# One line group moved in TensorE's order: the step's piece of projection between logits and row logits

## The chip, the cores and the metric

The kernel runs as one program on 1 core of a Trainium2 chip. The metric is the device time of one execution in microseconds (us), lower is better, given as the median of several runs.

## The reference, cut to what matters

A decoder layer on 8 batches of 256 rows with 512 columns: a retention layer, then a cross attention, then a mixture-of-experts feed forward, each with a layernorm in front and the residual added. All arithmetic is float32. The change lies in the cross attention alone:

```python
q = (x @ Wq).reshape(b, n, 32, 16)                 # x: the normalised rows
k, v = split(ctx @ Wkv)                            # 32 heads of 16
q, k = apply_axial_rope(q, pos), apply_axial_rope(k, pos)
w = softmax(einsum('bqhd,bkhd->bhqk', q, k) / 4)
attn = einsum('bhqk,bkhd->bqhd', w, v).reshape(b, n, 512)
x = x + attn @ Wout + bout
```

## The kernel before

The cross attention is a software pipeline written out by hand. Heads are worked two at a time: a batch g has 16 pairs p, and one pair is one **step**. An iteration b of the outer loop has T = 16 steps i, and in each step every engine does some work for up to four batches (`live` lists which). Iteration 0 starts batch 0 and prepares batch 1; iterations 1 to 6 are full; iteration 7 prepares no new batch; iteration 8 only drains.

What TensorE does, by function:

- `rows(g, p)` at step p: the row logits of a pair, four matmuls of 256 columns with 50 rows (L1254), into two banks of `b_rt`. VectorE's `maximum` reduces them to row maxima (L1471), and `rows` of the next step waits for that reduce.
- `logits(g, p)` 8 steps later (LAGS): the transposed logits with the maximum folded in (L1268), into the other two banks of `b_rt`. ScalarE's `exponentials` reads them (L1631), and the next `logits` waits for it.
- `values(g, q)`, 11 steps after the rows (LAGV), in odd steps: the products with v for four heads (L1281), copied out by ScalarE (`values_out`, L1624).
- `turn_values(g, q)`, one step later, in even steps: transposes of the result (L1289); VectorE's `group` divides by the sums and writes `b_attn` (L1491, L1493).
- `turn_maxima(g, k)`, in steps 4, 8, 12 and 0: transposes of the negated maxima (L1295); ScalarE copies them to `b_mT` (L1620) and DMAs place them beside q.
- `use(g, what, n, parts)`: one **piece** of a projection or of the output. `PLAN` says which piece stands in which step; step numbers are taken modulo 16, so all 16 steps of a full iteration have one. Step 4 has the two transposes of the normalised rows, `x0` and `x1` (L1311), step 5 `k1`, step 11 the two transposes of the attention result, `o0` and `o1` (L1339), step 12 `v0`. The others are parts of q, k, v and of the output w. The matmuls are made by `matmul3`, three fp32r products a term (L41, L42, L43).

All pieces share two PSUM banks, `b_gm`, in turns: w1, x0, k1, q1, o1, v1 in bank 0 and k0, x1, q0, o0, v0, w0 in bank 1. The first part of a piece waits for `gm_read` of its bank, that is, until the piece before it there has been read. The readers work in the following step: `take` on VectorE multiplies k and q by the rotary tables (L1461, twice), adds w to the residual (L1467) and forms the low parts `b_xl` of x and o (L1453) after ScalarE has written the high parts `b_xh` (L1594, L1599). `x0` waits besides for `xn_done`, the rows normalised by VectorE in steps 2 and 3 (L1441), and `o0` for `attn_done`, the last `group` of step 10.

The order within a step is fixed by the program of each engine. VectorE's is: `take` of the previous step's piece, `maximum`, `negate` (in steps 3, 7, 11 and 15), `group` (even steps), then statistics and `normalize`. ScalarE's is: `take`, `exponentials`, the high part of a rotated k or q, `maxima_out`, `values_out`. SyncE's queue issues the chunk loads of q and k, the maxima and the write-outs of the rotated rows, in steps of the same count.

Of the kernel before, what the change touches and what calls it, by code (L numbers as in the profile page):

```python
# [1021 lines left out]
def cross_attention(nc, X, Wa, Wb, first, csT, wb_dram, ctx_dram, bout_dram, pack_dram, ident, held, final, lead, ws_dram, gate_dram, const_dram, tri_dram):  # L1022
# [6 lines left out]
    with ExitStack() as mem:  # L1029
# [37 lines left out]
        def pb(name, shape):  # L1067
# [28 lines left out]
        PLAN = [(32, "w", 1, (0, 1)), (33, "w", 1, (2,)), (34, "w", 1, (3,)), (-14, "k", 0, (0,)), (-13, "k", 0, (1,)),  # L1096
# [16 lines left out]
        def uses(g, what, n):  # L1113

            place = [use[1:] for use in ORDER].index((what, n))
            ahead = ORDER[place][0] // T
            total, per = 0, 0
            for m, use in enumerate(ORDER):
                if m % 2 == place % 2:
                    more, done = ahead - use[0] // T + (m <= place), int(use[1] in AHEAD)  # L1120
                    if isinstance(g, int):
                        total += max(min(g + more, B) - done, 0)
                    else:
                        total, per = total + more - done, per + 1
            return total if isinstance(g, int) else g * per + total

        def due(i, live, step):

            return [d for d in live if i - d * T == step]

        def pairs(i, live, lag):
            return [(d, i - d * T - lag) for d in live if 0 <= i - d * T - lag < HP]

        def quads(i, live, lag):
            return [(d, (i - d * T - lag) // 2) for d in live if 0 <= i - d * T - lag < HP and (i - d * T - lag) % 2 == 0]
# [17 lines left out]
        def fresh(g):  # L1153
            return isinstance(g, int) and g <= 0

        def second(g):
            return isinstance(g, int) and g == 1
# [84 lines left out]
        def _(pe):  # L1242
# [14 lines left out]
            def logits(g, p):  # L1257

                k = p // 4
                if p % 4 == 0:  # L1260
                    pe.wait_ge(m_moved[k % 2], g * 128 + (k // 2 * 64 + 64))
                if fresh(g) and p == 0:
                    pe.wait_ge(mx_done, LAGS + 1)
                pe.wait_ge(e_done, g * HP + (p + 1))
                for j in range(TB):
                    for e in range(2):
                        r = slice(64 * e, 64 * e + 3 * XD + 2)
                        last = nc.tensor.matmul(rt[:, 2 + e, j * S:(j + 1) * S], kT[r, p, j * P:(j + 1) * P], qT[r, p, :], start=True, stop=True)  # L1268
                last.then_inc(st_mm, 1)
# [28 lines left out]
            def use(g, what, n, parts):  # L1298
                bank = BANK[what, n]
                out = gm[:, bank, :]  # L1300
                a = slice(n % 2 * P, (n % 2 + 1) * P)
                if 0 in parts:
                    earlier = uses(g, what, n) - 1
                    if not (isinstance(earlier, int) and earlier == 0):
                        pe.wait_ge(gm_read[bank], earlier)
                if what == "x":
                    if n == 0:
                        pe.wait_ge(xn_done, g)
                    rows_n = first.xn if second(g) else xn
                    for m in range(KT):  # L1310
                        last = nc.tensor.transpose(out[:, m * P:(m + 1) * P], rows_n[:, n, m * P:(m + 1) * P], ident[:, :])  # L1311
                elif what == "k":
                    if 0 in parts:
                        pe.wait_ge(cl_done, g)
                    for r in parts:
                        for m in range(CKT):
                            o = m * 2 * C + (2 * r + n) * P
                            last = matmul3(nc, out[:, r * S:(r + 1) * S], (wh[:, 1, o:o + P], wl[:, 1, o:o + P]),
                                           (ch[:, m, :], cl[:, m, :]), m == 0, m == CKT - 1)
                elif what == "q":  # L1320
                    if n == 0 and 0 in parts:
                        for t in range(TB):
                            pe.wait_ge(gm_read[BANK["x", t]], uses(g, "x", t))
                    for part in parts:
                        r = part // 2
                        for m in range(part % 2 * 2, part % 2 * 2 + 2):
                            o = m * C + (2 * r + n) * P
                            last = matmul3(nc, out[:, r * S:(r + 1) * S], (wh[:, 0, o:o + P], wl[:, 0, o:o + P]),
                                           (xh[:, m, :], xl[:, m, :]), m == 0, m == KT - 1)
                elif what == "v":  # L1330
                    for m in parts:
                        o = (2 * m + 1) * C
                        last = matmul3(nc, out, (ch[:, m, a], cl[:, m, a]), (wh[:, 1, o:o + C], wl[:, 1, o:o + C]),
                                       m == 0, m == CKT - 1)
                elif what == "o":
                    if n == 0:
                        pe.wait_ge(attn_done, g * 8 + 9)
                    for m in range(KT):
                        last = nc.tensor.transpose(out[:, m * P:(m + 1) * P], attn[:, n, m * P:(m + 1) * P], ident[:, :])  # L1339
                else:  # L1340
                    if 0 in parts:
                        pe.wait_ge(wl_done, 1)
                        pe.wait_ge(gm_read[BANK["o", n]], uses(g, "o", n))
                    for m in parts:
                        last = matmul3(nc, out, (ah[:, m, a], al[:, m, a]), (wh[:, 2, m * C:(m + 1) * C], wl[:, 2, m * C:(m + 1) * C]),
                                       m == 0, m == KT - 1)
                if PARTS[what] - 1 in parts:
                    last.then_inc(gm_mm[bank], 1)
# [35 lines left out]
            def body(b, live):  # L1384
                for i in range(T):
                    for d, p in pairs(i, live, LAGS):
                        logits(b + d, p)
                    for d, p in pairs(i, live, 0):
                        rows(b + d, p)
                    if isinstance(b, int) and b == 0 and i == 1:  # L1390
                        for n in range(8):
                            nc.tensor.transpose(nat[:, 0:P], ident[:, :], ident[:, :])
                    for d, q in quads(i, live, LAGV + 1):
                        turn_values(b + d, q)
                    for k in range(4):
                        for d in due(i, live, 4 * k + 4):
                            if not (fresh(b + d) and k == 0):
                                turn_maxima(b + d, k)
                        for d in due(i, live, 4 * k + 5):
                            pe.wait_ge(mt_done, (b + d) * 4 + (k + 1))  # L1400
                    if isinstance(b, int) and b == B and 4 <= i < 8:
                        lead_turn(i - 4)
                    if isinstance(b, int) and b == B and i == 10:
                        lead_router((0, 1))
                    for d, q in quads(i, live, LAGV):
                        values(b + d, q)
                    for step, what, n, parts in PLAN:
                        for d in due(i, live, step):
                            if not (fresh(b + d) and step < 0):
                                use(b + d, what, n, parts)  # L1410
                    if isinstance(b, int) and b == 0 and i == 4:
                        turn_maxima(0, 0)
                    if isinstance(b, int) and b == B and i == 11:
                        lead_router((2, 3))
                    if isinstance(b, int) and b == B and i == 12:
                        lead_turn_later(4)
                        lead_turn_later(5)
# [1320 lines left out]
```

## Time and profile before

| | us |
|---|---|
| median of 3 runs | 1372.47 (1368.34 to 1374.85) |
| the profiled execution, its time | 1369.42 |
| its span in the profile | 1367.6 |
| mean granted TensorE clock | 0.99 of full speed |
| TensorE busy with matmuls | 1329.1 |
| VectorE busy | 824.3 |
| ScalarE busy | 486.6 |

The cross attention runs from about 346.8 us of the span, where the first row logits start, to a little past 700 us. PE is TensorE's matmul, PEld its weight load, DVE VectorE, ACT ScalarE. Each matmul of the table of instructions overlaps the next, so a busy PE says that matmuls are in flight, not that the array is streaming all the time; the distance from one start to the next is what counts.

### The profile page before, as it was taken

How to read it: one execution, taken by the hardware profiler on the slowest of the kernel's cores; microseconds unless marked ns; L12 is line 12 of the kernel's file. 1: busy time of each engine (PE TensorE's matmuls, PEld its weight loads, DVE VectorE, ACT ScalarE, POOL GpSimd, SP SyncE). 2: the span in 40 equal slices, each digit the busy share in tenths (PEclk: the TensorE clock that was granted, in tenths of full speed). 3: DMA queues.
4: the chain of work that ended last, by engine and by line, in shares of the span. 5: the costliest groups of instructions: out<-in, count | busy, mean ns of one | idle time of the engine just before them, and what ended most of it. 6: DMA issues, size and time to landing. Idle time of an engine off the chain costs nothing. (4 is left out here: it accounts for less than half of the span.)

```text
span 1367.6 us, 24216 instructions
## 1 busy us (share of the span) xinstructions
PE 1329.1 (97%) x8490; PEld 1076.7 (79%) x8490; DVE 824.3 (60%) x1494; ACT 486.6 (36%) x765; POOL 519.9 (38%) x371
## 2 busy tenths in 40 slices
PE   8999999998889999999989999999999999999997
PEld 7777788877667777777568788888888899999986
DVE  6766667789777888888844657555531222222248
ACT  4222333334366665666665111111111232222220
POOL 1122222225543443344142018441133686555074
PEclk9999999999899999999999999999999999999999
DMA  7992000002655545555400003240010544443257
GB/s 273 321 327 104 0 0 0 0 9 94 185 163 167 173 144 152 157 150 172 126 1 23 24 24 146 85 150 24 23 39 1 195 148 143 143 175 111 85 172 245
DMA packets 85036, 159.85 MB, mean 117 GB/s; under 512 B 8576, under 2 KB 61952, under 8 KB 81536
## 3 DMA queue, kind: packets, MB, share of 16 engines
q1 hardware_dynamic: 78688, 124.19, 28.6%
q0 software_dynamic: 6272, 34.61, 7.1%
q8 instruction: 52, 0.85, 0.3%
q14 instruction: 24, 0.20, 0.1%
HBM read 109.22 MB, written 69.47 MB: 131 GB/s over the span
## 5 line engine op out<-in xcount | busy, mean ns | idle before, releaser
L1631 ACT ACTIVATE b_pf<-b_rt,b_zero 128x1024 f32<-128x1024 f32 x128 | 142.9, 1116 | 104.3 <-PE b_rt L1268 103.8
L1471 DVE TENSOR_REDUCE b_mx<-b_rt 128x4 f32<-128x1024 f32 x128 | 156.3, 1222 | 37.4 <-PE b_rt L1254 36.8
L2192 DVE SCALAR_TENSOR_TENSOR residual<-c_yp,c_shared,residual 128x512 f32<-128x512 f32 x128 | 92.3, 745 | 104.9 <-PE c_yp L43 100.8
L41 PE MATMUL c_fc<-c_xh,c_w 128*128 128x512 f32 x348 | 136.0, 391 | 0.0
L43 PE MATMUL c_fc<-c_xh,c_w 128*128 128x512 f32 x348 | 135.5, 389 | 0.0
L42 PE MATMUL c_fc<-c_xl,c_w 128*128 128x512 f32 x348 | 135.4, 389 | 0.0
L2358 ACT ACTIVATE c_s<-c_fc 128x512 f32<-128x512 f32 x43 | 25.7, 598 | 228.5 <-PE c_fc L43 217.4
L2206 DVE TENSOR_TENSOR c_hTl<-c_eh,c_hTh 128x384 fp32r<-128x384 f32 x39 | 21.8, 558 | 140.5 <-ACT c_hTh L2382 128.2
L41 PE MATMUL c_fc<-c_ring,c_xTl 128*128 x312 | 104.0, 333 | 0.0
L43 PE MATMUL c_fc<-c_ring,c_xTh 128*128 x312 | 100.7, 323 | 0.0
L42 PE MATMUL c_fc<-c_ring,c_xTh 128*128 x312 | 100.3, 322 | 0.0
L2003 POOL TENSOR_TENSOR c_w<-c_wraw,c_zero 128x1536 fp32r<-128x1536 f32 x9 | 24.7, 2749 | 197.3 <-DMA c_wraw<-in_c_ws 108.1
L2025 POOL TENSOR_TENSOR c_ring<-c_eraw,c_ring 128x2816 fp32r<-128x2816 f32 (+1 forms) x16 | 78.2, 4885 | 1.3
L2023 POOL TENSOR_TENSOR c_ring<-c_eraw,c_zero 128x2816 fp32r<-128x2816 f32 (+1 forms) x16 | 61.1, 3816 | 46.2 <-DMA c_eraw<-in_c_we 46.2
L43 PEld LDWEIGHTS c_fc<-c_xh,c_w 128*128 128x128 f32 x348 | 65.3, 188 | 13.6
L41 PEld LDWEIGHTS c_fc<-c_xh,c_w 128*128 128x128 f32 x348 | 65.3, 188 | 13.4
L42 PEld LDWEIGHTS c_fc<-c_xl,c_w 128*128 128x128 f32 x348 | 65.3, 188 | 13.3
L1268 PE MATMUL b_rt<-weights_b 50*128 50x256 f32 x512 | 65.1, 333 | 9.4 <-DMA weights_b<-b_mT 5.2
L1268 PEld LDWEIGHTS b_rt<-weights_b 50*128 50x128 f32 x512 | 38.6, 186 | 41.8 <-issue 20.9
L1281 PE MATMUL b_av<-b_pf,b_vp 128*32 128x256 f32 x1024 | 69.4, 389 | 0.0
L2388 ACT COPY c_ye<-c_ey 128x512 f32<-128x512 f32 x39 | 22.9, 587 | 119.5 <-PE c_ey L43 119.5
L41 PEld LDWEIGHTS c_fc<-c_ring,c_xTl 128*128 128x128 f32 x312 | 58.7, 188 | 3.5 <-issue 0.8
(451 smaller groups left out, 3543.2 us busy)
## 6 DMA issues: line engine op xcount, KB each, us to landing
weights_b<-b_pack SPq DMA_DIRECT2D x128, 200.0 KB
c_eraw<-in_c_we POOLq DMA_DIRECT2D x8, 2176.0 KB, 9.9
b_pack<-b_hi SPq DMA_DIRECT2D x56, 256.0 KB, 2.5
c_rows_in<-in_b_ctx SPq DMA_DIRECT2D x39, 256.0 KB, 10.3
c_rows_out<-in_b_ctx SPq DMA_DIRECT2D x39, 256.0 KB, 10.5
c_xe<-c_rows_in SPq DMA_DIRECT2D x39, 256.0 KB, 2.7
c_rows_out<-c_ye SPq DMA_DIRECT2D x39, 256.0 KB
c_wraw<-in_c_ws SPq DMA_DIRECT2D x11, 768.0 KB, 4.3
```

The costliest lines, as they stand in the source:

```text
L41: nc.tensor.matmul(out, ll, rh, start=start, stop=False)
L42: nc.tensor.matmul(out, lh, rl, start=False, stop=False)
L43: return nc.tensor.matmul(out, lh, rh, start=False, stop=stop)
L1268: last = nc.tensor.matmul(rt[:, 2 + e, j * S:(j + 1) * S], kT[r, p, j * P:(j + 1) * P], qT[r, p, :], start=True, stop=True)
L1281: last = nc.tensor.matmul(av[r:r + VW, 0:S], vp[:, j * XH + h, :], pf[:, h % 8, j * S:(j + 1) * S], start=j == 0, stop=j == TB - 1)
L1471: nc.vector.tensor_reduce(out=mx[:, :, 2 * p:2 * p + 2].rearrange("p t e -> p e t"), in_=rt[:, row_bank(g, p):row_bank(g, p) + 2, :].rearr ...
L1631: nc.scalar.activation(pf[:, s:s + 2, :], rt[:, 2:4, :], ACT.Exp, scale=XD ** -0.5, bias=zero[:, :]).then_inc(e_done, 1)
L2003: nc.gpsimd.tensor_tensor(w[k][:, 0, :], wraw[k][:, 1, :], zero[:, :].to_broadcast([P, PW]), ALU.add).then_inc(high_done, 1)
L2023: nc.gpsimd.tensor_tensor(high, raw, zero[:, :].to_broadcast([P, hi - lo]), ALU.add).then_inc(high_done, 1)
L2025: nc.gpsimd.tensor_tensor(low, raw, as_f32(high), ALU.subtract).then_inc(ew_done, 1)
L2192: nc.vector.scalar_tensor_tensor(out=X[:, t, :], in0=yp[:, (n * 4 + k) % 3, :], scalar=shared[:, t:t + 1], in1=X[:, t, :], op0=ALU.mult, o ...
L2358: nc.scalar.activation(s[:, n % 2, :], fc[:, n % 2, 0, :] if n else lead.products[:, 0, :], ACT.Silu).then_inc(s_done, 1)
```

## The change

In each step TensorE's `use` stands directly behind `logits` and ahead of `rows`, `turn_values`, `turn_maxima` and `values`. Before, it stood behind all of them. No instruction is added or removed on any engine, and no engine other than TensorE has another order.

```diff
                 for i in range(T):
                     for d, p in pairs(i, live, LAGS):
                         logits(b + d, p)
+                    for step, what, n, parts in PLAN:
+                        for d in due(i, live, step):
+                            if not (fresh(b + d) and step < 0):
+                                use(b + d, what, n, parts)
                     for d, p in pairs(i, live, 0):
                         rows(b + d, p)
                     if isinstance(b, int) and b == 0 and i == 1:
...
                     for d, q in quads(i, live, LAGV):
                         values(b + d, q)
-                    for step, what, n, parts in PLAN:
-                        for d in due(i, live, step):
-                            if not (fresh(b + d) and step < 0):
-                                use(b + d, what, n, parts)
                     if isinstance(b, int) and b == 0 and i == 4:
                         turn_maxima(0, 0)
```

## Rows read from the trace of the kernel before

**Rows 1.** The page: TensorE's busy time and granted clock

```profile
PE 1329.1 (97%) x8490; PEld 1076.7 (79%) x8490; DVE 824.3 (60%) x1494; ACT 486.6 (36%) x765; POOL 519.9 (38%) x371
PEclk9999999999899999999999999999999999999999
```

**Rows 2.** The waits of PE: us in total, times, longest

```profile
PE b_rt L1268 <- ACT b_pf L1631: 3.4, 7, 0.6
PE b_rt L1254 <- DVE b_mx L1471: 1.0, 3, 0.5
```

**Rows 3.** Timeline of PEld, steps 0 and 1: start, us, engine

```profile
562.86 0.30 PEld L1268 LDWEIGHTS b_rt<-weights_b 50*128 50x128 f32 x4 [0.37 <-issue]
...
563.52 0.20 PEld L1289 LDWEIGHTS b_nat<-identity,b_at 128*128 128x128 f32 x2
...
563.91 0.19 PEld L41 LDWEIGHTS b_gm<-weights_a,b_xl 128*128 128x128 f32 x1
...
565.50 0.30 PEld L1268 LDWEIGHTS b_rt<-weights_b 50*128 50x128 f32 x4 [0.36 <-issue]
565.73 0.30 PEld L1254 LDWEIGHTS b_rt<-weights_b 50*128 50x128 f32 x4
566.17 0.59 PEld L1281 LDWEIGHTS b_av<-b_pf,b_vp 128*32 128x32 f32 x16
567.17 0.19 PEld L41 LDWEIGHTS b_gm<-weights_a,b_xl 128*128 128x128 f32 x1 [0.41 <-issue]
...
568.06 0.30 PEld L1268 LDWEIGHTS b_rt<-weights_b 50*128 50x128 f32 x4 [0.36 <-issue]
```

**Rows 4.** Timeline of PEld in iteration 8, logits with no row logits behind

```profile
684.93 0.30 PEld L1268 LDWEIGHTS b_rt<-weights_b 50*128 50x128 f32 x4 [0.36 <-issue]
685.37 0.20 PEld L1289 LDWEIGHTS b_nat<-identity,b_at 128*128 128x128 f32 x2
```

**Rows 5.** Timeline of PEld, last transposes of step 4, logits of step 5

```profile
573.93 0.25 PEld L1295 LDWEIGHTS b_av<-identity,b_nm 128*128 128x128 f32 x2
...
574.93 0.42 PEld L1311 LDWEIGHTS b_gm<-identity,b_xn 128*128 128x128 f32 x4 [0.31 <-DVE b_bs L1461]
575.52 0.30 PEld L1268 LDWEIGHTS b_rt<-weights_b 50*128 50x128 f32 x4 [0.17 <-issue]
```

**Rows 6.** Timeline of DVE: reduce of step 1, then steps 3 to 5

```profile
566.29 1.23 DVE L1471 TENSOR_REDUCE b_mx<-b_rt 128x4 f32<-128x1024 f32 x1 [0.24 <-PE b_rt L1254]
...
571.50 1.21 DVE L1471 TENSOR_REDUCE b_mx<-b_rt 128x4 f32<-128x1024 f32 x1
...
573.59 0.69 DVE L1461 TENSOR_TENSOR b_ac<-b_gm,table 128x512 f32<-128x512 f32 x1
...
574.79 1.22 DVE L1471 TENSOR_REDUCE b_mx<-b_rt 128x4 f32<-128x1024 f32 x1
...
576.37 1.28 DVE L1453 TENSOR_TENSOR b_xl<-b_gm,b_xh 128x512 fp32r<-128x512 f32 x2
```

**Rows 7.** Timeline of ACT: steps 15 and 4

```profile
561.41 0.37 ACT L1624 COPY b_at<-b_av 128x256 f32<-128x256 f32 x1 [0.15 <-PE b_av L1281]
...
574.66 0.34 ACT L1620 CAST b_mT<-b_av 32x256 fp32r<-32x256 f32 x1
575.04 1.17 ACT L1594 CAST b_xh<-b_gm 128x512 fp32r<-128x512 f32 x2
```

**Rows 8.** Timeline of PE: two long waits for the maxima's DMAs

```profile
376.21 0.50 PE L1268 MATMUL b_rt<-weights_b 50*128 50x256 f32 x4 [2.18 <-DMA weights_b<-b_mT]
...
388.55 0.50 PE L1268 MATMUL b_rt<-weights_b 50*128 50x256 f32 x4 [3.01 <-DMA weights_b<-b_mT]
```

**Rows 9.** Windows: busy us of PE, PEld, DVE, ACT, POOL, clock, DMA

```profile
376.00:378.00 2.00, 1.78 (x15) 1.57 (x16) 1.00 (x1) 1.24 (x2) 0.00 (x0) 1.00 0.95 316
...
388.00:390.00 2.00, 1.45 (x11) 1.22 (x12) 0.54 (x1) 0.90 (x1) 0.00 (x0) 0.75 0.77 247
...
394.00:396.00 2.00, 2.00 (x13) 1.78 (x12) 1.36 (x3) 1.11 (x1) 1.88 (x2) 0.54 0.51 146
```

## The prediction

> **What bounds the kernel now.** I read the page first: TensorE is busy for 97% of the span, and its granted clock is at or near full in all forty slices [rows 1]. The change touches TensorE's order in the cross attention alone, so the question is what TensorE spends there. The view of the waits gives it little: 3.4 us on ScalarE's exponentials and 1.0 us on VectorE's maxima in the whole kernel [rows 2]. So TensorE sets the pace of the attention, and a step is as long as its TensorE work. What can make it longer is work that overlaps less, or new waits.
>
> Next the weight loads in order of time, since each opens a block of matmuls [rows 3]. Step 0 runs from 562.86 to 565.50 = 2.64 us, step 1 from 565.50 to 568.06 = 2.56 us. From the logits' first load to the transposes (563.52) are 0.66 us for logits and row logits together, from the transposes to the piece (563.91) 0.39 us, from the piece to the next logits 1.59 us. In step 1 the values take 1.00 us (566.17 to 567.17) and the piece 0.89 us. The piece is the last block of a step. Everything that VectorE and ScalarE do for it ahead of time has the whole step to be finished, and this is the reserve that the change spends.
>
> **First part: more switches between kinds of blocks.** No instruction goes or comes, but neighbours change. Logits and row logits have the same shape and flow into each other: 0.66 us for both. Logits followed by another kind take 0.44 us until the next load (684.93 to 685.37) [rows 4]; row logits followed by another kind take the same 0.44 us (565.73 to 566.17) [rows 3]. With the piece between them both pay it: together 0.86 to 0.88 us against 0.66, so 0.20 us more in each step. A piece behind logits costs what it costs behind values or transposes (0.89 and 1.59 us, first load to next load), I assume, and values behind row logits stay as they are. In even steps the transposes now stand directly before the next logits. Today the piece's loads run on from them (0.39 us for four transposes). A block of transposes before logits shows a gap: the last four transposes of step 4 load for 0.42 us, then 0.17 us pass, and logits load at 575.52 [rows 5]. So even steps pay 0.20 + 0.17 = 0.37 us. Eight even and eight odd steps: 8 x 0.37 + 8 x 0.20 = 4.6 us for a full iteration. The bounds are 0 (if the loads are pulled ahead, and I see no row of that here) and 16 x 0.37 = 5.9 us.
>
> The Trainium skill, "TensorE: Matmul & The Clock Gate", section "Step-by-step: what each phase is for", says that TensorE pulls weight loads ahead of matmuls in flight where row groups do not conflict or where the background weight buffer takes them. By that alone the switches would cost nothing, and the sum below would be about 30 us less. The rows disagree for this pair of shapes: before each logits behind a piece the loader is idle for 0.36 us.
>
> **Second part: pieces whose inputs come from the step before.** The piece is now wanted 0.43 us after the step's start. Row logits, and with them the reduce and all that VectorE has behind it, move to the far side of the piece, so the end of the chain moves later too. A chain of VectorE that begins with the reduce of the previous step can start about 0.55 us after the first load of the row logits (565.73 to 566.29) [rows 3, 6]. I count from that load, R, and compare it with the moment at which TensorE comes to the piece. A reduce takes 1.2, reduce and `group` 1.58 (574.79 to 576.37), `take` of k or q 1.20 (573.59 to 574.79), one half of `b_xl` 0.6 us [rows 6]. Four pieces of an iteration are late:
>
> - x1, step 4. It needs k0 read from bank 1. VectorE has reduce, `negate`, `normalize` and `take` k0 in a row: from the reduce at 571.50 to the load of x1 at 574.93 are 3.43 us [rows 5, 6], with no gap in it. The start is R + 0.55, or R + 1.1 if `take` of w1 is still ahead of it. So x1 can start at R + 4.0 to 4.5. TensorE arrives after row logits 0.43, values 1.00, logits 0.43 and x0 0.43, at R + 2.3. Stall 1.7 to 2.2; I take 2.0 us. `xn_done` of x0 lies inside this wait.
> - k1, step 5. It needs the low half of x0. ScalarE serves the maxima first: from their load to the copy 0.73 us and to the high part 1.11 us (573.93, 574.66, 575.04) [rows 5, 7]. These transposes load at R + 0.60, so the high part starts at R + 1.7 and is there at R + 2.3; with 0.6 for the low half, k1 can start at R + 3.0. TensorE arrives at R + 0.43 + 0.56 + 0.43 = 1.4. Stall 1.5 us.
> - o0 and o1, step 11. `group` of step 10 ends at R + 0.55 + 1.58 = 2.1, and o0 is wanted at R + 0.43 + 0.34 + 0.43 = 1.2. Behind `group` VectorE takes q1, 1.2 us, and only then bank 0 is free for o1: R + 3.45 against R + 1.6. Stall 1.8 us, the one of o0 inside it.
> - v0, step 12. It needs the low half of o0. ScalarE first copies out the values of step 11, which now end with the step: R + 1.43, then 0.14 until the copy starts (its row shows 0.15 of waiting) and 0.4 for the copy (0.37 and a little) [rows 7], 0.6 high, 0.65 low: R + 3.25 against R + 1.86. Stall 1.4 us.
>
> Together 6.7 us. For the other pieces the bank was last written two steps before, or the input is older; I find no wait there. Today's steps 4 and 5 already wait, 0.31 us for x1 [rows 5] and about as much for the maxima, and that is contained in the new stalls, so 0.7 us comes off. What is late next is the row logits of the same step, and VectorE idles for them; VectorE then has spare time, so this does not go on growing. SyncE's queue changes little: the maxima leave up to 1.5 us later in steps 5, 9, 13 and 1, and the logits that need them come three steps later.
>
> **The sum.** A full iteration: 6.7 - 0.7 + 4.6 = 10.6 us. Six of them (1 to 6; in iteration 1 the output pieces of two steps are missing, 0.6 us less): 63. Iteration 0 has six steps with all three blocks (1.9 us) and the stalls of x1 and k1, but two waits for DMAs of 2.18 and 3.01 us end near its last steps [rows 8] and can swallow part of it: 3 us, between 0 and 6. Iteration 7 has six pieces, 1.7 us, and o0 for about 1 us; the drain 0.4 us. Sum 63 + 3 + 2.7 + 0.4 = 69 us. On the profiled execution of 1369.4 us that is 1438; its time lies 3 us under the median of the three runs, and on the median it is 1441. I take 1439. A measurement of this kernel can tell 0.5%, some 7 us, from no change.
>
> **Rivals.**
> - The stalls also bring the clock down. The wait of 2.18 us before 376.21 left the granted clock at full speed (1.00 from 376 to 378); the one of 3.01 us before 388.55 was followed by windows at 0.75 down to 0.50 [rows 8, 9], the lower level of 1.2 GHz, until about 396. Six to seven us at half speed cost about 3.5. Once in an iteration is 6 x 3.5 = 21 us more, 1460; at all four places it would be over 1500. My longest gap is shorter than the one that left the clock alone, but four come in every iteration. The Trainium skill, same page, section "A second HAM failure mode: psum-queue depth-cycling", says that frequent short idling between groups of matmuls can make the clock oscillate; no row here shows it for gaps of this length.
> - The stalls are hidden and only the switches cost. That needs VectorE to be ahead by two us and more at steps 4 and 11. The rows speak against it, since its chain of steps 3 to 5 has no gap. It gives 1369 + 6 x 4.6 + 4 = 1401.
> - The switches cost nothing and only the stalls remain: 1369 + 6 x 6.0 + 4 = 1409. The idle loader before logits speaks against it.
> - Not slower. The row logits now come later, when the reduce of the previous step is surely over, and VectorE and ScalarE can read a piece while TensorE is at rows and values. What that can win is TensorE's waits on them, 3.4 + 1.0 us, with x1's 0.3 under 5 us: 1364, which would be measured as no change. It decides only if switches cost under 0.04 us a step and no piece is late. I see four that are.
>
> **How the numbers follow.** Forecast 0.62, with its own range 1415 to 1458; clock 0.13; stalls hidden 0.11; switches free 0.09; not slower 0.05. The range 1396 to 1466 takes in the second and third rival and the mild form of the first, and leaves out its strong form and the last. Slower by over 0.5% 0.94, within 0.5% 0.04 (nearly all of the last rival), faster 0.02.
>
> **What the profile after would show.** A full iteration about 10 us longer than before, 53 to 54 us where 16 steps of 2.6 to 2.7 us take 42 to 44 now. The waits of PE: on L1461 at the load of x1 near 2 us six or seven times, on L1453 at the first load of k1 and of v0 near 1.5 us each, on L1461 at o1. The loads of row logits 0.43 us ahead of values or transposes and the same from logits to the piece. VectorE's idle time before the reduce, on L1254, several times as large. In the windows of the attention TensorE busy falls from all but full to about 85%. A wait of PE on a line that I do not name, a clock under full speed in the middle of the attention, or iterations only 5 us longer would show me wrong: the first a chain that I overlooked, the second the clock, the third one of the two middle rivals.

## The result, and the profile after

The changed kernel takes 1462.16 us (median of 4 runs, 1456.29 to 1463.41), the kernel before 1370.81 us beside it: 1.065 times, 95% interval 1.062 to 1.068. The forecast of 1439 was 23 us short, inside its range of 1396 to 1466. The likeliest case was not quite what happened. It was that case together with the first rival.

The page, its share of busy time and the clock in forty slices, to be held against [rows 1]:

```profile
PE 1378.3 (94%) x8490; PEld 1094.0 (75%) x8490; DVE 823.7 (56%) x1494; ACT 487.5 (33%) x765; POOL 516.7 (35%) x371
PEclk9999999998998988899999999999999999999999
```

VectorE and ScalarE have the same instructions and, within 1 us, the same busy time. Busy time of TensorE grew by 49 us, and six slices between the 10th and the 20th show a clock under nine tenths, where before one did: the same matmuls, some at the lower level. The rest of the 94 us by which the span grew is idle time.

The view of TensorE's waits (us in all, times, longest), where [rows 2] had 4.4 us on two lines:

```profile
PE b_gm L41 <- DVE b_xl L1453: 16.1, 13, 1.7
PE b_gm L1311 <- DVE b_xn L1441: 9.7, 6, 1.8
PE b_gm L1339 <- DVE b_attn L1493: 6.4, 7, 1.1
PE b_gm L1311 <- DVE b_bs L1461: 5.5, 6, 3.3
PE b_rt L1268 <- ACT b_pf L1631: 5.1, 8, 1.0
...
PE b_rt L1254 <- DVE b_mx L1471: 3.2, 6, 1.1
PE b_gm L1339 <- DVE b_bs L1461: 3.2, 6, 0.5
```

The lines on `b_gm`, the pieces, are the forecast's four places and no others: k1 and v0 wait for `b_xl` 13 times, x0 for the normalised rows and x1 for the bank of k0, o0 for the last `group` and o1 for the bank of q1. They come to 41 us. Logits and row logits (`b_rt`) wait a little more too, 5.1 and 3.2 us where [rows 2] had 3.4 and 1.0.

The timeline of the weight loads in steps 14, 15, 3, 4 and 5 of one iteration, as in [rows 3, 5] (pieces' inner loads left out):

```profile
617.02 0.30 PEld L1268 LDWEIGHTS b_rt<-weights_b 50*128 50x128 f32 x4 [0.41 <-issue]
617.45 0.19 PEld L41 LDWEIGHTS b_gm<-weights_a,b_cl 128*128 128x128 f32 x1
...
619.70 0.30 PEld L1254 LDWEIGHTS b_rt<-weights_b 50*128 50x128 f32 x4 [0.35 <-issue]
620.13 0.20 PEld L1289 LDWEIGHTS b_nat<-identity,b_at 128*128 128x128 f32 x2
620.50 0.30 PEld L1268 LDWEIGHTS b_rt<-weights_b 50*128 50x128 f32 x4 [0.17 <-issue]
...
635.38 0.30 PEld L1268 LDWEIGHTS b_rt<-weights_b 50*128 50x128 f32 x4 [0.41 <-issue]
637.62 0.42 PEld L1311 LDWEIGHTS b_gm<-identity,b_xn 128*128 128x128 f32 x4 [1.95 <-issue]
638.76 0.42 PEld L1311 LDWEIGHTS b_gm<-identity,b_xn 128*128 128x128 f32 x4 [0.72 <-DVE b_bs L1461]
639.34 0.30 PEld L1254 LDWEIGHTS b_rt<-weights_b 50*128 50x128 f32 x4 [0.17 <-issue]
...
640.36 0.30 PEld L1268 LDWEIGHTS b_rt<-weights_b 50*128 50x128 f32 x4 [0.17 <-issue]
642.20 0.19 PEld L41 LDWEIGHTS b_gm<-b_ch,weights_a 128*128 128x128 f32 x1 [1.54 <-DVE b_xl L1453]
...
645.26 0.30 PEld L1268 LDWEIGHTS b_rt<-weights_b 50*128 50x128 f32 x4 [0.41 <-issue]
```

Logits to piece take 0.43 us, row logits to transposes 0.43, two transposes to the next logits 0.37, as forecast. Step 4 lasts from 635.38 to 640.36 = 4.98 us, step 5 until 645.26 = 4.90.

What VectorE does meanwhile, timeline of DVE in steps 3 and 4:

```profile
635.32 1.21 DVE L1471 TENSOR_REDUCE b_mx<-b_rt 128x4 f32<-128x1024 f32 x1
636.66 0.18 DVE L1482 TENSOR_SCALAR b_nm<-b_mx 128x16 fp32r<-128x16 f32 x1
...
636.97 0.54 DVE L1441 TENSOR_SCALAR b_xn<-residual,b_mv,b_rstd 128x512 f32 x1
637.42 0.69 DVE L1461 TENSOR_TENSOR b_ac<-b_gm,table 128x512 f32<-128x512 f32 x1
638.02 0.68 DVE L1461 TENSOR_TENSOR b_bs<-b_gm,table 128x512 f32<-128x512 f32 x1
639.89 1.23 DVE L1471 TENSOR_REDUCE b_mx<-b_rt 128x4 f32<-128x1024 f32 x1 [1.19 <-PE b_rt L1254]
```

The reduce of step 3 starts at 635.32 and x1 is released at 638.76, 3.44 us later; before it was 3.43 [rows 5, 6]. From there on the chain is the same, it only starts too late, and then VectorE idles 1.19 us for the row logits that stand behind x1.

The starts of all 128 logits give the length of each step. Full iterations at full clock (us):

| step | before | changed | | step | before | changed |
|---|---|---|---|---|---|---|
| 0 | 2.64 | 3.05 | | 8 | 2.83 | 3.08 |
| 1 | 2.56 | 2.77 | | 9 | 2.57 | 2.77 |
| 2 | 2.45 | 2.83 | | 10 | 2.46 | 2.86 |
| 3 | 2.57 | 2.77 | | 11 | 2.69 | 4.68 |
| 4 | 2.43 | 4.98 | | 12 | 2.75 | 4.39 |
| 5 | 3.60 | 4.90 | | 13 | 2.57 | 2.76 |
| 6 | 2.47 | 2.86 | | 14 | 3.12 | 3.48 |
| 7 | 2.57 | 2.77 | | 15 | 3.27 | 3.46 |

Twelve steps are 3.4 us longer together, by 0.2 (odd) or 0.25 to 0.4 us (even). The four with late pieces are 7.5 us longer. That is 10.8 us an iteration (54.4 against 43.6), where the forecast had 10.6.

What is missing is the clock. Steps 4 and 5 were slower still in four of the six full iterations. The windows about one such place (busy us of PE, PEld, DVE, ACT, POOL; then clock, DMA share, GB/s):

```profile
514.00:518.00 4.00, 2.13 (x24) 0.98 (x16) 3.83 (x8) 1.49 (x2) 0.00 (x0) 0.93 0.64 171
518.00:522.00 4.00, 3.60 (x16) 2.43 (x16) 1.80 (x4) 0.78 (x3) 1.41 (x2) 0.50 0.11 24
522.00:526.00 4.00, 3.16 (x14) 2.94 (x16) 1.29 (x2) 2.06 (x4) 1.28 (x1) 0.50 0.17 56
526.00:530.00 4.00, 4.00 (x36) 2.58 (x34) 2.42 (x3) 1.49 (x2) 0.96 (x2) 0.79 0.41 144
```

The stall before x0 had just ended:

```profile
517.12 0.78 PE L1311 MATMUL b_gm<-identity,b_xn 128*128 128x128 f32 x4 [1.77 <-DVE b_xn L1441]
```

From about 517.5 to 527.7 (worked out from the shares 0.93 and 0.79 of the outer windows) the clock was granted at one half, 1.2 GHz. Steps 4 and 5 of this iteration took 13.2 us instead of 9.9. In two iterations step 11 was slow as well, in one of them step 12 too, and the waits there were far shorter:

```profile
543.83 0.66 PE L1339 MATMUL b_gm<-identity,b_attn 128*128 128x128 f32 x4 [0.96 <-DVE b_attn L1493]
545.02 1.12 PE L1339 MATMUL b_gm<-identity,b_attn 128*128 128x128 f32 x4 [0.54 <-DVE b_bs L1461]
545.00:547.00 2.00, 1.98 (x12) 1.42 (x16) 0.09 (x1) 0.00 (x0) 1.41 (x2) 0.50 0.29 106
```

### The profile page after: what moved, and what is told of

Read it like the earlier page. It is cut to its first block and busy times, and to the rows that moved or that the text cites. A ratio compares the mean times of both kernels' runs of the same rounds, so it can differ in the third digit from the quotient of the medians.

```text
span 1461.6 us, 24218 instructions
## 1 busy us (share of the span) xinstructions
PE 1378.3 (94%) x8490; PEld 1094.0 (75%) x8490; DVE 823.7 (56%) x1494; ACT 487.5 (33%) x765; POOL 516.7 (35%) x371
## 5 line engine op out<-in xcount | busy, mean ns | idle before, releaser
L1268 PEld LDWEIGHTS b_rt<-weights_b 50*128 50x128 f32 x512 | 39.8, 192 | 48.6 <-issue 36.4
L1268 PE MATMUL b_rt<-weights_b 50*128 50x256 f32 x512 | 66.5, 339 | 8.8 <-ACT b_pf L1631 5.1
L1254 PE MATMUL b_rt<-weights_b 50*128 50x256 f32 x512 | 68.2, 347 | 5.7 <-DVE b_mx L1471 3.2
L1281 PE MATMUL b_av<-b_pf,b_vp 128*32 128x256 f32 x1024 | 73.4, 407 | 0.0
L1254 PEld LDWEIGHTS b_rt<-weights_b 50*128 50x128 f32 x512 | 41.3, 200 | 35.4 <-issue 20.7
## 6 DMA issues: line engine op xcount, KB each, us to landing
c_rows_in<-in_b_ctx SPq DMA_DIRECT2D x39, 256.0 KB, 10.6
```

Of the source, the lines that this page charges most:

```text
L1254: last = nc.tensor.matmul(rt[:, row_bank(g, p) + e, t * S:(t + 1) * S], qT[r, p, t * P:(t + 1) * P], kT[r, p, :], start=True, stop=True)
L1281: last = nc.tensor.matmul(av[r:r + VW, 0:S], vp[:, j * XH + h, :], pf[:, h % 8, j * S:(j + 1) * S], start=j == 0, stop=j == TB - 1)
```

## The experiments

Each kernel ran in rounds with the kernel before on the same chip. Ratios are to that kernel; its median was between 1365 and 1371 us. Step lengths are taken from the starts of the logits, as above.

**Twelve pieces moved, four left (e1).** The pieces of steps 4, 5, 11 and 12 stay at the end of their step.

```diff
+        LATE = (4, 5, 11, 12)
...
                         logits(b + d, p)
+                    for step, what, n, parts in PLAN:
+                        for d in due(i, live, step):
+                            if not (fresh(b + d) and step < 0) and (step % T not in LATE):
+                                use(b + d, what, n, parts)
...
-                            if not (fresh(b + d) and step < 0):
+                            if not (fresh(b + d) and step < 0) and (step % T in LATE):
```

> The pieces of twelve steps stand between logits and row logits, those of steps 4, 5, 11 and 12 stay at the end of their step. My theory (switches between kinds of blocks cost by themselves, stalls come only at the four): no new waits and no lower clock, but 8 odd or even steps pay 0.20 and 0.37 us, 3.5 us in a full iteration, some 23 us in all, so about 1394 us. Rival (the switches are hidden and all of the loss is stalls and clock): within 5 us of 1371.

Measured: 1402.99 us, 1.0257 times (1.0231 to 1.0283). The kernel before took 1367.01 us beside it, so the twelve cost 36 us, where my theory had 23 and the rival at most 5. The twelve steps have to a hundredth the lengths of the changed kernel, so 3.4 us an iteration is what the switches cost where nothing waits. The other 13 us are something that I had not thought of. Between step 3, whose piece is early, and step 4, whose piece is late, no piece stands between two row logits, and they come too fast for VectorE. The loads of step 4:

```profile
598.03 0.30 PEld L1269 LDWEIGHTS b_rt<-weights_b 50*128 50x128 f32 x4 [0.41 <-issue]
599.23 0.30 PEld L1255 LDWEIGHTS b_rt<-weights_b 50*128 50x128 f32 x4 [0.90 <-DVE b_mx L1476]
...
601.39 0.69 PEld L1312 LDWEIGHTS b_gm<-identity,b_xn 128*128 128x128 f32 x4 [0.72 <-DVE b_bs L1466]
```

Step 4 became 1.5 us, step 11 0.8 us and step 12 0.4 us longer through this. Switching costs are confirmed, and "nothing waits" was wrong for a mixed order. "No lower clock" was wrong too. In two of the six full iterations steps 4 and 5 took 8.8 us instead of 7.6. The windows behind the loads above, which belong to one of them:

```profile
601.00:603.00 2.00, 1.60 (x8) 1.28 (x10) 1.97 (x5) 1.06 (x2) 1.41 (x2) 0.61 0.26 62
603.00:605.00 2.00, 2.00 (x23) 0.94 (x20) 2.00 (x3) 1.73 (x3) 0.04 (x1) 0.53 0.01 4
```

The matmuls had waited 0.70 us for the maxima and 0.48 us at x1, nothing longer (the loader's 0.90 and 0.72 us count from its own last load).

**Four pieces moved, twelve left (e2).** The same with `in` and `not in` exchanged.

> Only the pieces of steps 4, 5, 11 and 12 are moved. My theory: 6.0 us of net stall and 1.1 us of switches in each of six iterations, some 5 us at the ends, and the clock falls to its lower level after some of the stalls as in the changed kernel, 20 us more: about 1438 us. Rival (the clock falls for another reason, such as the many short gaps at the twelve other places): no stretch at the lower level beyond those of the kernel before, 1419 us.

Measured: 1409.89 us, 1.0319 (1.0294 to 1.0345): 43 us, less than either theory. Step 4 took 3.45 us and not 4.98, because step 3 now ends with its piece and TensorE comes to x0 later, and step 11 likewise 3.47 and not 4.68. Steps 5 and 12 took 4.90 and 4.38 us as in the changed kernel, and step 13 0.6 us more than before for the mixed order. That is 5.4 us an iteration at full clock (49.0 against 43.6). In three of six iterations step 5 took 6.35 to 6.39 us, the lower clock again. So the clock does fall with these four alone, though less often.

**Twelve pieces at the very front (e3).** As e1, with the twelve ahead of the logits.

```diff
                 for i in range(T):
+                    for step, what, n, parts in PLAN:
+                        for d in due(i, live, step):
+                            if not (fresh(b + d) and step < 0) and (step % T not in LATE):
+                                use(b + d, what, n, parts)
                     for d, p in pairs(i, live, LAGS):
                         logits(b + d, p)
```

> As the first of these, but the twelve pieces stand ahead of the logits, at the very front of their step, so logits and row logits touch again and the piece is wanted even earlier. My theory (what costs there is the parting of the two, not the early place): 1371 us, within 5. Rival (a piece early in its step costs something at every step, by waits or by work pushed behind it): 1385 us or more.

Measured: 1392.57 us, 1.0191 (1.0159 to 1.0222). The total missed my 1371 and falls into the rival's range. The steps say why. Steps 6 to 9 have only moved pieces, and they take 1.75 + 3.37 + 1.97 + 3.29 = 10.4 us, as before (10.4) and unlike the changed kernel (11.5): with logits and row logits touching again, the switching cost is gone. What costs is the seam, as in e1: steps 3 and 4 together take 6.6 to 7.2 us in iterations 2 to 6 (5.0 before, and with one piece more in them), with waits of row logits for the reduce of up to 1.6 us. Behind these waits the clock fell in four of six iterations, which are 47.3 to 49.4 us long where the one after them has 46.9. The place in the step costs nothing by itself; an order that differs from step to step does.

**Work in the stalls (e4).** The changed kernel with matmuls ahead of the four late pieces.

```diff
+                                if step in (-12, -11, 27, -4) and n == (what == "k") and 0 in live and not fresh(b):
+                                    pe.wait_ge(mx_done, b * HP + (i + 1))
+                                    for _ in range(9):
+                                        nc.tensor.matmul(rt[:, 0, 0:S], wh[:, 0, 0:P], wh[:, 0, 0:S], start=True, stop=True)
                                 use(b + d, what, n, parts)
```

> The changed kernel with nine idle-time matmuls of 256 columns, 1.1 us together, ahead of the late piece in steps 4, 5, 11 and 12 of iterations 1 to 7 (their results are overwritten by the row logits). They wait for the maxima of the step before, so that their bank is free, which is over well before the piece's own input is there. My theory: the four stalls bring the clock down, and with work in them it stays up; 20 us faster than the changed kernel, about 1440 us. Rival (the clock has no part in it, the stalls are simply longer than forecast): no gain, 1462 us or slightly more.

Measured: 1434.91 us, 1.0502 (1.0468 to 1.0536). More matmuls made it 20 us faster than the change, by the two ratios. The windows of the attention, filled kernel:

```profile
420.00:500.00 80.00, 77.52 (x637) 53.42 (x640) 52.53 (x96) 40.47 (x59) 24.54 (x24) 1.00 0.43 127
500.00:580.00 80.00, 76.64 (x657) 54.62 (x650) 55.40 (x103) 39.52 (x57) 26.32 (x27) 1.00 0.40 120
580.00:660.00 80.00, 77.52 (x642) 53.75 (x640) 54.13 (x104) 40.93 (x59) 26.30 (x27) 1.00 0.45 131
```

and of the changed kernel:

```profile
420.00:500.00 80.00, 71.61 (x568) 48.18 (x566) 49.25 (x85) 38.77 (x57) 24.27 (x24) 0.94 0.44 130
500.00:580.00 80.00, 72.19 (x539) 47.73 (x539) 53.00 (x104) 36.10 (x50) 23.39 (x24) 0.87 0.38 110
580.00:660.00 80.00, 72.61 (x584) 49.68 (x582) 50.76 (x91) 38.32 (x55) 26.29 (x28) 0.92 0.39 115
```

In iterations 2 to 6 all late steps now have the length of the table above within 0.05 us, and these iterations are 54.5 us each, where the changed kernel has 57.4, 61.3, 59.2, 54.4 and 54.4. One stretch at the lower clock is left behind them, in iteration 7 (0.83 from 740 to 750 us).

**Only the wait (e9),** the control: `range(0)` in place of `range(9)`.

> The control for the filled kernel: the changed kernel with the same added wait for the maxima of the step before at the four late pieces, but no matmuls behind it. My theory (the matmuls keep the clock up, the wait is nothing): as the changed kernel, 1.065 times before, about 1460 us, with stretches at the lower clock in the attention. Rival (the added wait itself orders things better): as the filled kernel, 1.050 times.

Measured: 1456.63 us, 1.0687 (1.0646 to 1.0728). Iterations 2 to 6 are again 61.4, 59.2, 54.4, 54.4 and 57.4 us long. These are the lengths of the changed kernel's iterations, in another order. So the wait alone does nothing, and it is the matmuls that keep the clock up.

**All pieces first, filled (e5).** The loop over `PLAN` with the four added lines of e4 stands ahead of the logits.

> The filled kernel, but with every piece at the very front of its step, ahead of the logits, so that logits and row logits touch again and the pieces of steps 4, 5, 11 and 12 are wanted 0.43 us earlier still. My theory: the parting of logits and row logits with its switches costs 4.6 us in a full iteration, the four longer stalls give 4 x 0.43 = 1.7 us of it back, net 2.9 us x 6 = 17 us faster than the filled kernel, 1.038 times the kernel before, about 1420 us. Rival (switches cost nothing): 10 us slower than the filled kernel, 1.057 times the kernel before, about 1446 us.

Measured: 1438.04 us, 1.0497 (1.0464 to 1.0530), the same as e4 and between the two expectations. Steps 6 to 9 take 10.4 us, so the switching cost is gone here too. Iteration 4, the only one from 2 to 6 that stays at full clock, takes 52.9 us where e4 has 54.5: 1.6 us won, forecast 2.9. So the stalls grew by more than the 0.43 us that I added to each. From the logits of step 3 to those of step 4, which now include x0 and x1, are 6.6 to 7.5 us in iterations 2 to 6. The added matmuls themselves stand behind a wait for the maxima of up to 2.0 us:

```profile
PE b_rt L1393 <- DVE b_mx L1476: 22.9, 25, 2.0
```

So they leave the first part of the stall empty, and the clock fell in four of the six full iterations; these take 53.8 to 54.8 us. From iteration 1 on the attention is 4.0 us shorter than in e4. In these two executions what lies ahead of it and behind it is 2.5 and 3.3 us longer, and such stretches vary by more than that between executions of one order (see the ends, below). The total alone could not have told the theories apart.

**VectorE's order mended for k0 and the rows (e6).** TensorE as changed.

```diff
                     for step, what, n in ENDS:
-                        for d in due(i, live, step + 1):
+                        for d in due(i, live, step + (what in ("x", "o"))):
                             if not (fresh(b + d) and step < 0):
                                 take(b + d, what, n)
+                    for t in range(TB):
+                        for d in due(i, live, -14 + t):
+                            if not fresh(b + d) and not second(b + d):
+                                normalize(b + d, t)
                     for d, p in pairs(i, live, 0):
                         maximum(b + d, p)
...
-                    for t in range(TB):
-                        for d in due(i, live, -14 + t):
-                            if not fresh(b + d) and not second(b + d):
-                                normalize(b + d, t)
```

> TensorE's order as changed; VectorE takes k, q and w in the step of the piece itself instead of the next one, and normalises, both ahead of the reduce. My theory: the stall of x0 and x1 in step 4 (2.5 us) is VectorE's chain behind the late reduce, so it goes to under 0.5 us; k1, o0 and v0 keep theirs. 2.2 x 6 = 13 us, and one fewer cause for the lower clock, some 5 us: about 1444 us, 1.054 times before. Rival (the chain is not what x1 waits for, or the reduce becomes late by as much): within 5 us of the changed kernel, 1.065 times.

Measured: 1454.32 us, 1.0627 (1.0596 to 1.0658), barely better than the change and by the total the rival's case. The chain was what x1 waited for, but the gain went elsewhere, as the rival's second half had it. The waits of TensorE:

```profile
PE b_gm L41 <- DVE b_xl L1454: 16.3, 13, 1.7
PE b_gm L1340 <- DVE b_attn L1494: 11.0, 7, 1.8
PE b_rt L1255 <- DVE b_mx L1472: 9.6, 10, 1.8
...
PE b_gm L1312 <- DVE b_xn L1442: 1.9, 5, 0.4
```

The wait for the rows went from 9.7 to 1.9 us, the one of x1 for its bank is gone, and step 4 fell from 4.98 to 2.95 us. But the reduce of step 2 now stands behind w1's `take` and `normalize` and is late, so that the row logits of step 3 wait 0.7 to 0.9 us, and the take of q1 ahead of the reduce of step 10 delays the last `group`: o0 waits 11.0 us in all, where o0 and o1 together had 9.6. Step 11 keeps its 4.68 us in one of six iterations, and is 6.2 us or more in the others. One wait, 1.93 us for the loader and 1.7 us for the matmuls, has taken the place of two shorter ones, and the clock falls behind it:

```profile
593.73 1.47 PEld L1340 LDWEIGHTS b_gm<-identity,b_attn 128*128 128x128 f32 x8 [1.93 <-DVE b_attn L1494]
```

```profile
592.00:594.00 2.00, 0.28 (x4) 0.27 (x3) 1.65 (x4) 1.11 (x1) 1.61 (x3) 0.97 0.94 323
594.00:596.00 2.00, 2.00 (x12) 1.67 (x10) 0.00 (x0) 0.00 (x0) 0.00 (x0) 0.50 0.19 71
```

The first is the load of o0 and o1, the second the windows around it.

**Steps 4 and 5 alone (e7), steps 11 and 12 alone (e10).** As e2 with `LATE = (4, 5)` and `(11, 12)`.

> Only the pieces of steps 4 and 5 are moved. My theory: x1 2.0 and k1 1.5 us of stall less 0.7 of today's waits, 0.57 us of switches, 3.4 us in each of six iterations and 3 us in iteration 0: 23 us, 1392 us, and steps 11 and 12 would account for the other 20 of the 43 us that the four cost together. Rival (the cost of the four is mostly in one pair): under 10 or over 35 us.

> Only the pieces of steps 11 and 12 are moved, the other half of the four. The step lengths of the kernel with all four moved say 0.8 us more in step 11, 1.6 in step 12 and 0.6 in step 13, 3.0 x 6 = 18 us, and 2 to 3 us in iteration 7: 1391 us, 1.015 times before. Rival (the pairs do not add up, since each needs the other's delay or the clock): under 1.010 or over 1.022.

Measured: 1393.91 us, 1.0175 (1.0145 to 1.0205), and 1386.03 us, 1.0153 (1.0132 to 1.0175). Against the kernel before beside them that is 23 and 21 us, as forecast. For e7 the agreement is in part luck: at full clock an iteration is 2.4 us longer and not 3.4, since step 4 takes 3.45 us as in e2, and the lower clock makes up for it. Together the two cost 3.3%, and the four together cost 3.2%: they add. With steps 4 and 5 moved, step 5 took 6.1 to 6.4 us in four of six iterations; with 11 and 12 moved iterations 2 to 6 are 46.5 us each and none slows. So the stalls at x1 and k1 are enough to bring the clock down. But the longest wait does not rank the cases. The matmuls waited 0.36 us at o1 and 1.27 at v0 in e10, and the clock never fell; they waited 0.70 and 0.48 us in e1, and it fell twice.

**The kernel before, warmed (e8).** What e4 taught, applied to the kernel before.

```diff
+                if fresh(g) and p == 8:
+                    pe.wait_ge(e_done, g * HP + (p + 1))
+                    for _ in range(18):
+                        nc.tensor.matmul(rt[:, 2, 0:S], wh[:, 0, 0:P], wh[:, 0, 0:S], start=True, stop=True)
                 if p % 4 == 0:
                     pe.wait_ge(m_moved[k % 2], g * 128 + (k // 2 * 64 + 64))
...
                 for i in range(T):
+                    if isinstance(b, int) and b == 0 and i == 0:
+                        for n in range(14):
+                            nc.tensor.matmul(nat[:, 0:S], wh[:, 0, 0:P], wh[:, 0, 0:S], start=True, stop=True)
```

> The kernel before with matmuls of 256 columns put into two waits for DMAs: 14 where the attention begins and 18 ahead of the logits that wait 3.0 us at the start of iteration 1. Their results are overwritten or not used. The clock theory: the two stretches at the lower level in iteration 0 and 1, 20 us together, go away; TensorE is not alone the bound there, so 4 us faster, 0.997 times before. Rival (idle time has no part in the clock, or these stretches are bound by DMAs): 0 to 2 us slower.

Measured: 1366.69 us, 0.998 (0.9965 to 0.9996) over 12 runs. It is faster than the kernel before by no more than 0.2%, with an interval that barely leaves out no change. Iteration 1 is 42.2 us instead of 43.6, and the first eight logits steps 1.3 us shorter together. The loads at the former wait of 3.0 us [rows 8]:

```profile
384.52 2.21 PEld L1263 LDWEIGHTS b_rt<-weights_a 128*128 128x128 f32 x18 [0.41 <-ACT b_pf L1638]
387.19 0.30 PEld L1272 LDWEIGHTS b_rt<-weights_b 50*128 50x128 f32 x4 [0.46 <-DMA weights_b<-b_mT]
```

The cause is not shown. The stretch at the lower clock from 389 to 396 is gone, and the one from about 348 to 362 is half as long (the clock from 350 to 360 us is 0.73, before 0.50). But in e10, which has no added matmuls and the order of the kernel before in these steps, the first is gone too (1.00 from 380 to 400) and the other is as short (0.72). A new stretch in iteration 7 took back 1.4 us.

## Why the prediction was right, and where it fell short

- **TensorE sets the pace.** Right: every step is as long as its blocks and its stalls.
- **Switches, 4.6 us an iteration.** Confirmed by e1, e3 and the step table: 0.20 us in odd steps; 0.36 to 0.41 in even steps, but only 0.25 in step 8, where the kernel before already waited a little. Twelve steps give 3.4 us against 3.5 worked out. By the Trainium skill's rule on pulled-ahead loads ("TensorE: Matmul & The Clock Gate", "Step-by-step: what each phase is for") there would have been no cost, and the step table shows one. But the sign by which I refuted the rule was misread. The loader was not idle for 0.36 us before each logits behind a piece: in the kernel before that holds in six steps of sixteen, and in the others it was idle for 0.13 to 0.17 us. In the changed kernel row logits behind a piece show the same two values, and steps with 0.13 us (3, 7, 9) cost the same 0.20 us. The distance from load to load shows the cost; the loader's idle time does not.
- **Four late pieces, 6.7 us of stall.** Right in place, order and cause, and slightly small: with their switches the four steps cost 7.5 us, forecast 6.0 net and 1.1. The term off most is x1, taken as 2.0: step 4 grew by 2.55 us, where 2.0 less 0.3 of today's wait and 0.37 of switching gave 2.1. The row logits of step 3 load at R = 633.94, TensorE is ready for x1 at R + 2.3 as worked out, and x1 loads at 638.76 = R + 4.8, outside my 4.0 to 4.5. The reduce of step 3 started not at R + 0.55 or R + 1.1 but at R + 1.4: the reduce of step 2 had itself been late, and `group`, `normalize` and w1 stood behind it. I had followed the chain back by one step, and it needed two. The sums for k1 (1.5), o1 (1.8) and v0 (1.4) hit the growth of their steps within 0.2 us.
- **The full iteration** at full clock: 54.4 us against 43.6, 10.8 and 10.6 forecast. TensorE's busy share there is 89% (660 to 740 us), forecast 85%. Filled and before, iterations 1 to 6 differ by 61.8 us, forecast 63.
- **The ends.** Iteration 0, up to the end of its steps, cost 3.6 us (3), a match by luck: e4 and e9 have the same order there, and the same moment came at 389.4 and 388.0 us of their spans, 0.8 us after the kernel before and 0.5 us ahead of it. Iteration 7 cost 6.4, forecast 2.7: steps 13 and 14 there are 3.1 us longer, partly at the lower clock, steps 0 to 3 1.8 us and steps 11 and 12 1.2 us. Behind the last logits the span was 4.2 us longer than before. In the eleven other profiled executions, the kernel before among them, that stretch varied between 666.0 and 673.2 us without relation to the order, so I count it as scatter, and it made up 4 of the 23 us by which the forecast was short.
- **The step that failed** is the sentence "My longest gap is shorter than the one that left the clock alone", and the 0.13 given to the clock for it. The clock fell directly behind a wait of 1.77 us, in e6 behind one of 1.7, in the changed kernel's step 11 between waits of 0.96 and 0.54, and in e1 with no wait longer than 0.70 us in front. A clock under full speed in the middle of the attention was one of the signs that the prediction itself had named. The changed kernel's iterations 1 to 6 are 17.4 us longer than the filled ones, where the mild form of that rival had 21, which made it 1460. One row with a long gap that did no harm is no bound. The range held because this case had been priced into it, while the forecast's own range of 1415 to 1458 missed. What decides stays open: equal stalls of one kernel brought the clock down in some iterations and not in others, and no run here varied their moment alone. The Trainium skill, same page, "A second HAM failure mode: psum-queue depth-cycling", describes frequent short idling that makes the clock oscillate; the runs here agree so far, in that all falls in the full iterations stand at waits of 2 us or less, and in that e4 keeps the clock up through iterations 1 to 6 with 1.1 us of matmuls in each gap.
- **The other rivals.** "Stalls hidden" and "switches free" are each refuted by the step table. Of the last one a trace is real: the row logits of step 5 no longer wait 0.3 us for the reduce. In all, though, TensorE's waits for exponentials and maxima, which this rival had priced at up to 4.4 us of gain, rose from 4.4 to 8.3 us.

## What to carry to other kernels

In a pipeline written out by hand, a block at the end of a step is not only filler: everything that other engines make for it in the same step has the step's length as its reserve. Before such a block is moved, count for each variant of it how long the chain behind the previous release is, and compare with the work that stands in between. Keep blocks of one shape together, and look at the clock after every new stall: a stall can be paid a second time if the array slows behind it.

## What the hardware showed that I had not expected

- Parting two blocks of four 50-row matmuls by a block of full-array matmuls costs 0.20 us of TensorE time, though no instruction is added (0.66 us together, 0.86 apart).
- Behind a wait of 1.77 us the granted clock was one half for some 10 us, in some iterations and not in others of the same kernel; behind one of 2.18 us it had stayed full [rows 8, 9]. Behind waits of 0.70 and 0.48 us (e1) it fell in two of six iterations, behind 0.36 and 1.27 (e10) in none.
- Nine matmuls of no use in each of the four stalls made the kernel 1.5% faster; in e5, where they themselves came up to 2.0 us late, the clock fell in four of six iterations all the same.
